# Four attention-like layers over 8,192 tokens on one core: 64x64 weighted sums, biases added to x by VectorE, norm and value products in two steps, a finer merge of two slots

## Time and profile before

| what | value |
|---|---|
| median of 3 runs | 2071.68 us |
| span of the profiled execution, first to last instruction | 2068.7 us |
| TensorE (PE) busy | 1916.0 us, 93%, 21934 matmuls |
| VectorE (DVE) busy | 1272.5 us, 62% |
| ScalarE (ACT) busy | 957.6 us, 46% |
| GpSimd (POOL) busy | 157.4 us, 8% |
| mean granted TensorE clock | 0.978 |
| DMA | 30.45 MB, mean 15 GB/s |

### The profile page before, as it was taken

One profiled execution on the slowest core, in us unless ns is written; L12 is line 12 of the kernel. 1 busy time (PEld: TensorE's weight loads), 2 busy tenths in 40 slices (PEclk: granted clock), 3 DMA queues, 4 the chain that ended last, 5 costly groups with the idle time before them and its releaser, 6 DMA issues.

```text
span 2068.7 us, 53790 instructions
## 1 busy us (share of the span) xinstructions
PE 1916.0 (93%) x21934; PEld 1720.2 (83%) x21934; DVE 1272.5 (62%) x3513; ACT 957.6 (46%) x3544; POOL 157.4 (8%) x169
## 2 busy tenths in 40 slices
PE   7599999999999999999999999999999999999997
PEld 6488888888888888888888888888888888888886
DVE  3466666666666666566666666666666666656663
ACT  3344544544554544454554454454454454454452
POOL 0000000000000000000000000000000000000000
PEclk8699999999999999999999999999999999999998
DMA  6000000000000000000000000000000000000000
GB/s 190 1 3 13 13 12 13 7 8 13 13 12 11 13 2 13 13 12 12 12 3 12 13 13 11 13 3 12 13 12 11 13 3 12 13 13 11 12 7 6
DMA packets 36517, 30.45 MB, mean 15 GB/s; under 512 B 11568, under 2 KB 36144, under 8 KB 36336
## 3 DMA queue, kind: packets, MB, share of 16 engines
q1 hardware_dynamic: 36336, 27.55, 4.5%
HBM read 19.15 MB, written 8.39 MB: 13 GB/s over the span
## 4 chain that ended last, share of the span: by engine, by line
PE 86%; DVE 5%; ACT 5%; issue 3%; DMA 1%; POOL 0%; SPq 0%; POOLq 0%; DVEq 0%; ACTq 0%
PE ps L445 79%; PE ps L518 4%; PE ps L594 3%; ACT probs L792 3%; DVE probs L1006 1%; DVE small L918 1%; DVE x L1015 1%; ACT oT L802 1%; ACT hT L767 1%; PE ps L714 1%; DMA raw_mats<-mats 1%; DVE small L1004 0%; DMA x<-x 0%; POOL small L422 0%; DVE xn L936 0%
## 5 line engine op out<-in xcount | busy, mean ns | idle before, releaser
L445 PE MATMUL ps<-hT,w_hi 128*128 128x256 f32 x2560 | 500.2, 289 | 11.9 <-ACT hT L767 11.7
L445 PEld LDWEIGHTS ps<-hT,w_hi 128*128 128x128 f32 x2560 | 412.6, 192 | 29.5 <-ACT hT L767 24.1
L445 PE MATMUL ps<-w_hi,hT 128*128 128x256 f32 (+1 forms) x1536 | 430.2, 344 | 0.0
L792 ACT ACTIVATE probs<-probs,small 128x64 f32<-128x64 f32 x1024 | 341.4, 335 | 102.4 <-DVE small L996 101.8
L445 PE MATMUL ps<-hT,w_lo 128*128 128x256 f32 x1280 | 338.9, 285 | 0.0
L445 PEld LDWEIGHTS ps<-w_hi,hT 128*128 128x128 f32 x1536 | 272.5, 189 | 39.9 <-issue 6.5
L445 PE MATMUL ps<-w_lo,hT 128*128 128x256 f32 (+1 forms) x768 | 250.9, 338 | 0.0
L445 PEld LDWEIGHTS ps<-hT,w_lo 128*128 128x128 f32 x1280 | 245.6, 192 | 0.7
L422 POOL TENSOR_TENSOR small<-small,consts 128x2 f32<-128x2 f32 x128 | 94.1, 736 | 1669.2 <-DVE small L928 1669.1
L445 PE MATMUL ps<-w_hi,oT 128*128 128x256 f32 x768 | 183.5, 305 | 28.0 <-DVE oT L857 28.0
L792 ACT ACTIVATION_READ_ACCUMULATOR probs<-probs,small 128x1 f32 x1024 | 192.5, 188 | 0.0
(11 more groups left out here) (105 smaller groups left out, 3377.2 us busy)
## 6 DMA issues: line engine op xcount, KB each, us to landing
raw_mats<-mats SPq DMA_DIRECT2D x8, 1024.0 KB, 11.9
x<-x SPq DMA_DIRECT2D x32, 256.0 KB, 2.8
out<-xn SPq DMA_DIRECT2D x32, 256.0 KB, 2.9
adj<-adjq SPq DMA_DIRECT2D x64, 16.0 KB, 2.0
adjT<-adjt SPq DMA_DIRECT2D x64, 8.0 KB, 1.8
raw_consts<-board_consts SPq DMA_DIRECT2D x1, 515.5 KB, 3.6
w_bias<-rows SPq DMA_DIRECT2D x1, 256.0 KB, 5.3
bias_cols<-cols SPq DMA_DIRECT2D x1, 6.0 KB, 3.9
```

The costliest lines, as they stand in the source:

```text
L445: return nc.tensor.matmul(o, lhsT, rhs, start=start, stop=stop, skip_group_check=True)
L792: last = fn(p, p, ACT.Exp, bias=ROWMAX[s][:, row:row + 1], accum_out=ROWSUM[s][:, row:row + 1])
```

## The change

- `av`: the 64x128 products are cut in two 64x64 ones, ordered so that neighbours use different halves of the array; twice as many instructions
- the matmuls that added the v and output biases are gone. The value bias of attention 0 is multiplied by its output matrix once in the setup and joined with the output bias (BOB); a new DVE step `bias` adds BOB to x after the norm has read it, once per attention, and `out` waits for it
- the row terms: u_vec holds high and low parts side by side in 100 columns, so `r` has four matmuls for six; their results lie by board parity, so POOL expands half as much (R4 128x512 for 128x1024) and `s2` starts with two matmuls for four. ACT and DVE each take them out in two instructions for one
- norm by token halves: `stats` and `norm` are a step per token tile, with a POOL power for each; `transposed_h` turns one token tile per step
- value products in two steps: heads are paired anew in attention 0, and `heads` i waits for half i of the transposed probabilities
- smaller turns: `q`, `k`, `v`, `e`, `wh` and `ha` are two TensorE steps each; the list has 145 steps, and ORDER is new (lag 56 on TensorE). With PE's lists spelled out, the stretch of attention 1 in slot 0 and attention 2 in slot 1 is: before `scores1, turn2 x2, q2, k2, v2, pt1 x2, scores2, heads1, out1 x2, pt2 x2, heads2, turn3 x2, out2 x2`; after `scores1, turn2 x2, q2 x2, k2.0, pt1.0, k2.1, v2.0, heads1.0, v2.1, pt1.1, scores2, heads1.1, out1.0, pt2.0, out1.1, heads2.0, pt2.1, heads2.1, out2.0, turn3 x2, out2.1`; then `r3`

```diff
-ATT = [dict(layer=0, heads=8, mats=0, bias=1), dict(layer=1, heads=4, mats=4, bias=2),
-       dict(layer=3, heads=4, mats=8, bias=3)]
+ATT = [dict(layer=0, heads=8, mats=0), dict(layer=1, heads=4, mats=4), dict(layer=3, heads=4, mats=8)]
...
-HEADS_AT = [((0, 4), (1, 5), (3, 2), (6, 7)), ((0, 1), (3, 2)), ((0, 1), (3, 2))]
+HEADS_AT = [((0, 1), (2, 3), (5, 4), (7, 6)), ((0, 1), (3, 2)), ((0, 1), (3, 2))]
...
+        def norm_steps(a):
+            return ([("bn", a, 0), ("stats", a, 0), ("bn", a, 1), ("stats", a, 1), ("norm", a, 0), ("norm", a, 1)]
+                    + [("masks", a, 0)] * (a == 0) + [("turn", a, 0), ("turn", a, 1)])
...
+            for u in us:
+                softmax += [("mask", a, u), ("max", a, u)]
+            softmax += [("exp", a, u) for u in us[:half + 1]] + [("soft", a, u) for u in us[:half]]
+            softmax += [("pt", a, 0)] + [("exp", a, u) for u in us[half + 1:]] + [("heads", a, 0)]
+            softmax += [("soft", a, u) for u in us[half:]] + [("pt", a, 1), ("pv", a, 0), ("heads", a, 1), ("pv", a, 1)]
+            return (norm_steps(a) + [("bias", a, 0)] + [(k, a, i) for k in ("q", "k", "v") for i in range(2)]
+                    + [("scores", a, 0)] + softmax + [("out", a, 0), ("out", a, 1)])
...
-                    nc.gpsimd.tensor_tensor(RSTD[s], VE[s], HALF.broadcast_to([P, TT]), ALU.pow
-                                            ).then_inc(sm["rstd"], 1)
+                    nc.gpsimd.tensor_tensor(RSTD[s][:, i:i + 1], VE[s][:, i:i + 1], HALF, ALU.pow).then_inc(sm["rstd"], 1)
...
+            for n in range(3):
+                o = PS[:, 5 + n // 2, n % 2 * D:n % 2 * D + D]
+                last = mm(o, SELR[:, 1, :], RAWROWS[:, (n + 1) * D:(n + 1) * D + D], True, n > 0)
+                if n == 0:
+                    pe.wait_ge(raw_sems[0], 48)
+                    for c in range(DC):
+                        mm(o, BVB[:, c, :], RAWM[:, 3, c, :], False, c == DC - 1)
+            last.then_inc(setup["bo_ps"], 1)
...
-                if bias is not None:
-                    last = mm(o, SELR[:, 1, :], ROWS[:, bias * D:bias * D + D], False, True)
...
-                    pe.wait_ge(sm["pt_sb"], v.six[2 * a + 1])
+                    pe.wait_ge(sm["pt_sb"], v.six[2 * a + i])
...
-                        mm(o, UVEC[:, 0, c, :], HT[s][:, 0, c, :], c == 0, False)
-                        mm(o, UVEC[:, 1, c, :], HT[s][:, 0, c, :], False, False)
...
+                            last = mm(o, UVEC[:, c, :], HT[s][:, j, c, :], j == 0 and c == 0, j == 1 and c == DC - 1)
...
-                        for b in range(NB):
-                            t, e = divmod(b, 2)
-                            mm(bank(s, S2_BANKS[t])[:, 0:TOK], SELR[:, 3 + e, :], R4[s][:, b * TOK:b * TOK + TOK],
-                               e == 0, False)
+                        for t in range(TT):
+                            mm(bank(s, S2_BANKS[t])[:, 0:TOK], SELR[:, 3, :],
+                               R4[s][:, t, :, :].rearrange("p h q -> p (h q)"), True, False)
...
-                        for e in range(2):
-                            last = mm(bank(s, AV_BANKS[i][e])[:, m * SQ:m * SQ + SQ],
-                                      WH[s][SQ * e:SQ * e + SQ, i, m * P:m * P + P],
+                        for e, f in ((0, 0), (1, 1), (0, 1), (1, 0)):
+                            last = mm(bank(s, AV_BANKS[i][e])[SQ * f:SQ * f + SQ, m * SQ:m * SQ + SQ],
+                                      WH[s][SQ * e:SQ * e + SQ, i, m * P + SQ * f:m * P + SQ * f + SQ],
                                       A[s][SQ * e:SQ * e + SQ, i, h * SQ:h * SQ + SQ], True, True)
...
+                elif k == "bias":
+
+                    x = X[s][:, :].rearrange("p (t d) -> p t d", t=TT)
+                    dve.wait_ge(sm["xn_ready"], norm_halves(a, v)[1])
+                    tt(x, x, BOB[:, a:a + 1, :].broadcast_to([P, TT, D]), ALU.add).then_inc(sm["x_bias"], 1)
...
+                    dve.wait_ge(sm["x_bias"], n)
```

More of the change, by code:

```diff
@@ L84, in constants @@
     c[[1, 3, 5], C_SELAB + 1] = 1
[L85 to L90, removed]
+    for e in range(2):
+        for part in (SQ * e, SQ * e + H2, SQ * e + LO):
+            rows = np.arange(part, part + H2)
+            c[rows, C_HEADS + rows - part] = 1
+            c[rows, C_RT + SQ * e:C_RT + SQ * e + SQ] = 1
     c[:, C_HALF] = -0.5
@@ L298, in norm_halves @@
             return v.eight[2 * NORM_OF[a]:2 * NORM_OF[a] + 2]
+        def norm_steps(a):
+            return ([("bn", a, 0), ("stats", a, 0), ("bn", a, 1), ("stats", a, 1), ("norm", a, 0), ("norm", a, 1)]
+                    + [("masks", a, 0)] * (a == 0) + [("turn", a, 0), ("turn", a, 1)])
         def att_steps(a):
             us = units(a)
+            half = len(us) // 2
             softmax = []
-            for i in range(len(us) + 1):
-                softmax += [("mask", a, u) for u in us[i:i + 1]] + [("max", a, u) for u in us[max(i - 1, 0):i]]
@@ L486, in _ @@
             pe.wait_ge(raw_sems[5], 16)
+            pe.wait_ge(setup["bv"], 1)
             for ic in range(DC):
@@ L534, in features_out, with tokens_out @@
                 return last
-            def tokens_out(o, actT, t, m, bias=None, start=True, ready=(), halves=()):
+            def tokens_out(o, actT, t, m, start=True, ready=(), halves=()):
                 at = slice(t * P, t * P + P)
@@ new lines, in l2 @@
+                    t, pair = divmod(n, 2)
+                    if c == 0:
+                        if t == 0:
+                            pe.wait_ge(sm[("e_act", "e_dve")[n]], v.two[0])
+                        else:
+                            pe.wait_ge(sm["wh_sb"], v.four[n - 2])
+                    m = M_W + 2 * pair
+                    last = split3(bank(s, WH_BANKS[n]),
+                                  [(HT[s][:, 0, c, t * P:t * P + P], HT[s][:, 1, c, t * P:t * P + P],
+                                    WHI[:, m:m + 2, c, :], WLO[:, m:m + 2, c, :])], c == 0, c == DC - 1)
@@ L655, in l2 @@
+                    if c == DC - 1:
+                        last.then_inc(sm["wh_ps"], 1)
                 elif k == "s2":
@@ L762, in _ @@
             split_hi(4, len(SPLITS))
+            act.wait_ge(setup["bo_ps"], 1)
+            fn(BOB[:, 0:2, :], PS[:, 5, :], ACT.Copy)
+            last = fn(BOB[:, 2, :], PS[:, 6, 0:D], ACT.Copy)
+            last.then_inc(setup["bo_sb"], 1)
             act.wait_ge(setup["terms_zero"], 1)
@@ L814, in l2 @@
                     act.wait_ge(sm["r_ps"], n)
-                    fn(RS[s][0:RH, :], bank(s, 1)[0:RH, 0:TOK], ACT.Identity, bias=S0[:, :]
-                       ).then_inc(sm["r_hi"], 1)
-                elif k == "e" and i % 2 == 0:
-                    act.wait_ge(sm["e_ps"], v.four[i])
+                    for e in range(2):
+                        own = slice(SQ * e, SQ * e + LO + H2)
+                        last = fn(RS[s][own, :, :], r_view(s, e)[own, :, :], ACT.Identity, bias=S0[own, :])
+                    last.then_inc(sm["r_hi"], 1)
+                elif k == "e" and i % (2 * DC) == DC - 1:
+                    h = i // DC
+                    act.wait_ge(sm["e_ps"], v.four[h])
                     for oc in range(DC):
-                        last = fn(e_view(s, oc, i), e_bank(s, E_BANKS[i], oc), ACT.Identity, bias=CVEC[:, oc, i:i + 1])
+                        last = fn(e_view(s, oc, h), e_bank(s, E_BANKS[h], oc), ACT.Identity, bias=CVEC[:, oc, h:h + 1])
                     last.then_inc(sm["e_act"], 1)
@@ L875, in _ @@
             dve.wait_ge(setup["zeroed"], 1)
-            for part in (0, LO):
+            for part in range(0, P, LO):
                 nc.vector.tensor_copy(BPAD[:, :, part:part + H2].rearrange("p c h -> p h c"),
```

277 lines of the change are left out of this document (140 added, 137 removed), and 38 rows, old and new, of the table ORDER.

## The result

The changed kernel takes 2048.69 us, the median of four runs (2038.83 to 2054.13), against 2071.49 us of four runs of the kernel before on the same chip: a ratio of 0.9889 (0.9858 to 0.992). It is 1.1% faster, 23 us where 75 were forecast, and above the range of 1945 to 2045 us. Its four runs go by the clock: granted 0.980, 0.972, 0.968 and 0.966 with 2038.83, 2044.55, 2052.83 and 2054.13 us. The last is the profiled one. The kernel before was profiled at 0.978.

What follows compares the result with a forecast made beforehand. TensorE matmul time was taken as the bound (busy 93% of the span). Span 2068.7 - 89 (matmuls) + 18 (waits) - 4 (ramp, tail, setup) = 1993.7 us, plus 3 to the median: 1997 us; range 1965 to 2025, chance 0.55.

Steps and rivals of the forecast that it cites:

- covered stretch: Some 30 us per half iteration, layer 2 of one slot covering the other's attention 0, no idle: savings count in full.
- `r`, 7.7 us of the 89: Matmuls against u_vec: six become four per group, 0.12 us each, taking 7.7 us off.
- `av`, -41.6 us: Weighted sums in 64x64 products at 20 ns each: 0.65 us less per step, 64 steps, 41.6 us.
- Row terms and fold, -47.4 us: Removed matmuls: bias 30.7 us, `r` 7.7 us, row terms in `s2` 9.0 us.
- Rival 4: Bias matmuls are hidden between longer waits, so the fold shortens nothing and only `av` counts: 2044 us; chance 0.07.
- Waits, +1.2 us per iteration: TensorE idle grows with thinner filler in the tight stretch and something for the bias step: +18 us over 15 iterations.
- my reading of the tight stretch: 27.4 us with slots in attentions 1 and 2 holds all 3.3 us idle; `pt` waits stay largest after the change.
- More than 9 us idle per iteration: Sign on TensorE: idle above 9 us per iteration would make the forecast wrong upwards.
- Ramp and tail, -4 us: One-slot pass at the ends: -3 from halved norms and value products, -2 from half-clock matmuls, +1 setup.
- Rivals 1: Smaller pieces keep both slots apart, waits per iteration fall to about 3.3 us: 1929 us; chance 0.15.
- Rival 2: Bias steps and thinner filler put the softmax on the path, +4 us per iteration: 2039 us; chance 0.20.
- rival 3: Each cut `av` product costs a full 60 ns, +122 us: 2161 us; decides from 39 ns per instruction; chance 0.03.

Runs made afterwards that it cites:

- e4: Kernel before with all three cuts (64x64 `av` products, row terms, folded bias), old order, norm and value products kept: 2053.81 us, ratio 0.9921.
- e13: Kernel before plus ten needless matmuls between the two probability transposes of attention 2: 2062.89 us, ratio 0.9977.
- e14: Kernel before with the 64x64 `av` products and ten needless matmuls between attention 2's probability transposes: 2023.86 us, ratio 0.9788.
- e1: Kernel before with only the `av` products cut into 64x64, its own order kept: 2059.46 us, ratio 0.9958.
- e12: Changed kernel without the VectorE adds of the bias to x, those biases left out of the result: 2046.96 us, ratio 0.9899.
- e17: Changed kernel with eight needless matmuls ahead of attention 2's first probabilities wait and u_vec padded to 128 columns: 2031.13 us, ratio 0.9810.
- e9: Kernel before with only the second of each group's two `av` steps cut into 64x64 products: 2067.31 us, ratio 0.9997.
- e16: Kernel before with all three cuts, old order, ten needless matmuls in attention 2's `pt` wait, u_vec padded to 128 columns: 2014.25 us, ratio 0.9739.
- e10: Kernel before with all three cuts, old order, ten needless matmuls in attention 2's `pt` wait, u_vec at 100 columns: 2016.82 us, ratio 0.9745.

## Why the prediction was wrong

The likeliest case was 1997 us. Step by step:

- **The step that failed: matmul time saved in the covered stretch "comes out in full".** The sum takes all 89 us off the span, adds 1.2 us of waits per iteration, and has no term for the clock behind a wait. The runs showed two things in its place: the clock took back most of `av` (39.0 us with the clock held, 7 to 9 without), and waits took back most of the other two cuts even with the clock held (9.6 of 47 us left). The matmul times themselves were right or low: `av` fell from 1.93 to 1.09 us per step (1.28 forecast), the bias matmuls are gone, and the adds take 0.68 us (0.69 forecast). Only `r`, 7.7 us of the 89, was no cut in the new order, where it waits for its activations; the sum priced it at the old order's pace. A shorter stretch of matmuls was to be a shorter iteration, and per iteration 5.6 us became 0.74 under the old order (e4) and 0.6 with the new one.
- **`av`, -41.6 us: right in size with the clock held, partly by luck, and otherwise taken back by the clock.** The matmul time fell by 64 x 0.84 = 54 us, more than I priced, and stops that I did not foresee took some 11 of them. Filled, e13 to e14, it gives 39.0 us; unfilled, e1, about 7 to 9. I had the granted clock of every window before me and put it at 0.99 for good; half clock was to me a matter of the ramp alone.
- **Row terms and fold, -47.4 us: nearly nothing even with the clock held**, 9.6 us, of which the iterations have 0.31 x 15 = 4.7 and the two ends the rest; the fold's share of it, 2.0 us, is not clear of the noise. Rival 4, "the fold does not shorten anything", had this right, for the fold and the row terms alike. That its 2044 us is close to the measured 2048.7 is luck: it had `av` count in full, which it did not, and it missed the clock.
- **Waits, +1.2 us per iteration: 2.6 measured.** My walk through the new list got single ones: the `pt` behind the first `out` waits 1.52 us for 1.5 forecast, in this timeline of the changed kernel, and the issue wait is 0.52.

```profile
1131.77 0.44 PE L613 MATMUL ps<-consts,probs 128*128 128x128 f32 x2
1132.72 0.46 PE L453 MATMUL ps<-probsT,v 64*64 64x64 f32 x16 [0.52 <-issue]
1134.71 0.44 PE L613 MATMUL ps<-consts,probs 128*128 128x128 f32 x2 [1.52 <-DVE probs L1047]
...
1138.01 0.46 PE L453 MATMUL ps<-probsT,v 64*64 64x64 f32 x16 [0.52 <-issue]
```

  It missed that the issue wait ahead of `heads` comes more often now that there are two `heads` steps (45 waits of 0.52 us for 30, 7.8 us more; the other 11 us are further stops, of up to 1.2 us), and all of the wait for the normalised x, 2 us per iteration, outside the stretch that I walked through. There VectorE's second norm instruction waits for its power and then runs beside POOL:

```profile
1087.78 0.41 DVE L972 TENSOR_SCALAR xn<-x,small 128x256 f32<-128x256 f32 x1
1088.57 1.05 POOL L436 TENSOR_TENSOR row_terms<-rs,consts 128x512 fp32r<-128x512 f32 x1
1088.63 1.13 DVE L972 TENSOR_SCALAR xn<-x,small 128x256 f32<-128x256 f32 x1 [0.44 <-POOL small L432]
```

- **"If pt waits are not the largest after the change, my reading of the tight stretch is wrong":** from 112.5 to 1950 us they are not, issue is, 34.4 for 31.4; over the whole span they still are, 43.6 for 39.3. So that sign says little. "More than 9 us idle per iteration" (139.0 / 15 = 9.3) pointed where it should.
- **Ramp and tail, -4 us:** 7.4 measured, between two single executions. Rivals 1 and 3 fell. Rival 2 (2039 us) had 4 us of waits more per iteration where 2.6 came, and laid them to the bias steps and the softmax; the waits for probabilities shrank, and e12 clears the adds.
- **Two small slips in the working.** The 3 us from span to median compares the median with another run's span; each run stands only some 2 us above its own (2054.13 for 2052.2). And by its own terms rival 3 turns at 38 ns per instruction, not 39. Neither matters for the outcome.

The bookkeeping in times: 2062.9 (before, filled) - 39.0 (`av`) - 7.6 (row terms) - 2.0 (fold) + 16.9 (order and splits) = 2031.2, and + 17.6 for what the changed kernel loses without the filling and the 128 columns is its 2048.7. The terms are differences of neighbours in one chain, so they add up by construction; what is shown is their sizes. Not settled: how much of e17's 16.9 us, beyond the 14 that `r` takes longer there, is the order and how much a filling that fits less well; which chain of waits sets the iteration once the clock is held; and that the stops are code loading, which rests on their packets and on e9, not on a run that changes the code alone. A kernel that beats both the kernel before and the changed one is e16, 2014.25 us (e10 is level with it): the three cuts, the old order, and ten needless matmuls in a wait.

## What to carry to other kernels

Before counting a cut of matmul time as gain, look at the granted clock beside the waits in the same stretch: work removed around a wait can lower the clock behind it, and needless matmuls inside that wait are a cheap test of it and, here, the remedy. And price a matmul where it will stand: the four of `r` take 0.47 us in the old order and 0.8 to 1.0 in the new one, which puts them too soon behind what they read. Run a cut once with the clock held and once without, since otherwise a real gain looks like none. And time cut just ahead of a wait for another engine is not gained; ask of each removed matmul which wait ends next behind it.

## What the hardware showed that was not expected

- **Less work, lower clock.** The wait of 1.42 us ahead of `pt` is the longest in the stretch of e4 shown above, and its granted clock fell to 0.50 for 3.3 us all the same; 1.2 us of matmuls per 1.4 us wait in the same place of e10 kept the window's clock at 1.00, worth 37 us in 2054.
- **Two products of 64x64 cost less than one of 64x128:** 17 ns each against 60 ns, 1.09 us per step for 1.93, so cutting in two is 1.8 times faster. But TensorE then stands 1.1 to 1.8 us, without a semaphore, in 11 of 15 iterations.
- **A POOL instruction holds up VectorE:** a norm instruction takes 0.41 us alone and 1.13 to 1.25 us in all 31 cases in which it lies beside POOL's expansion of 1.05 us, and it ends 0.15 us after the expansion each time. Beside POOL's power, in 113 cases, it takes 0.40 to 0.41. The Trainium skill, "SBUF — State Buffer", section SBUF: two separate sides, says that the port pair shared by the two is an exclusive lock for certain VectorE instructions, and that whichever starts first has it for its whole instruction. The rows agree that VectorE waits for the expansion's end. They don't show the rule on who is first: in 15 of the 31 the profile has VectorE start 0.05 us ahead of POOL, and still VectorE is the one that waits.
